# Three PSUM banks for scores and two for row maxima in a macaron block

## The reference

```python
x = x + 0.5 * ffn(layernorm(x), W_up, W_gate, W_down)      # 256 -> 1024 -> 256
x = x + attn(layernorm(x), Wq, bq, Wk, bk, Wv, bv)
x = x + 0.5 * ffn(layernorm(x), W_up, W_gate, W_down)

def ffn(x, W_up, W_gate, W_down):           # weights ternary: clip(round(W/s), -1, 1) * s, s = mean|W|
    return (silu(x @ up.T) * (x @ gate.T)) @ down.T

def attn(x):                                # 16 heads of 16, 4 key/value groups, causal
    q, k, v = ...                           # k and v shared by the 4 heads of a group
    scores = q @ k.T / sqrt(16), -inf above the diagonal
    return softmax(scores) @ v
```

## Time and profile before

| | |
|---|---|
| time, median of 3 runs | 612.36 us (611.18 to 612.61) |
| span of the profiled execution | 610.4 us (its own time is not given beside it; median minus span is 2.0 us) |
| PE busy | 566.9 us, 93% |
| DVE busy | 485.1 us, 79% |
| ACT busy | 411.1 us, 67% |
| POOL busy | 184.6 us, 30% |
| TensorE clock granted | 0.997 of full, mean over the span |

### The profile page before, as it was taken

How to read it: one execution, slowest core, us unless ns; L and a number is a source line. 1 busy time by engine, 2 the same in 40 slices (tenths; PEclk the granted TensorE clock), 3 DMA queues, 4 the chain that set the end, 5 groups by cost and what they waited for, 6 DMA issues and landing times.

```text
span 610.4 us, 12447 instructions
## 1 busy us (share of the span) xinstructions
PE 566.9 (93%) x4276; PEld 346.0 (57%) x4276; DVE 485.1 (79%) x1854; ACT 411.1 (67%) x776; POOL 184.6 (30%) x231
## 2 busy tenths in 40 slices
PE   2869999999989989999899989998899999999998
PEld 2336566555656855656565656554445655666665
DVE  6998978989866889888988987888298687856654
ACT  4637765765635368898889888887866656665741
POOL 3115101110510234555545454557731011101100
PEclk9999999999989999999999999999999999999999
DMA  8601001100205161414141424230111111211112
GB/s 317 207 18 36 18 19 35 35 19 18 36 8 119 24 134 55 91 54 91 55 90 56 91 62 88 84 58 4 36 35 34 53 53 36 69 50 56 35 35 70
DMA packets 71679, 37.90 MB, mean 62 GB/s; under 512 B 33984, under 2 KB 71104, under 8 KB 71616
## 3 DMA queue, kind: packets, MB, share of 16 engines
q1 hardware_dynamic: 71616, 37.11, 23.9%
HBM read 18.22 MB, written 10.49 MB: 47 GB/s over the span
## 4 chain that ended last, share of the span: by engine, by line
PE 79%; DVE 12%; ACT 6%; issue 2%; DMA 1%; DVEq 0%
PE bank L1107 32%; PE bank L1119 17%; PE bank L1206 7%; PE bank L1270 6%; PE bank L1261 5%; PE bank L1233 5%; PE bank L1284 2%; PE bank L1275 2%; DVE hl L847 2%; ACT shared L587 2%; DVE sm_out L969 2%; DVE hid L832 2%; DVE stats L711 1%; PE bank L1098 1%; PE bank L1244 1%
## 5 line engine op out<-in xcount | busy, mean ns | idle before, releaser
L969 DVE CUSTOM_DVE_ANT_0 sm_out<-bank,mask 128x256 f16<-128x256 f32 (+1 forms) x512 | 153.0, 352 | 28.3 <-PE bank L1233 26.4
L477 ACT ACTIVATE silu<-bank,w_scale 128x512 f32<-128x512 f32 x128 | 87.3, 682 | 117.5 <-PE bank L1107 117.5
L832 DVE SCALAR_TENSOR_TENSOR hid<-silu,h_unit,bank 128x512 f32<-128x512 f32 x128 | 95.0, 742 | 63.4 <-ACT silu L477 63.2
L587 ACT ACTIVATE shared<-bank,qk_scale 128x512 f32<-128x512 f32 x192 | 121.2, 675 | 22.7 <-PE bank L1261 22.0
L1119 PE MATMUL bank<-wT_down,hh 128*128 128x256 f16 x512 | 118.7, 273 | 5.5 <-DVE hl L847 5.3
L1119 PE MATMUL bank<-wT_down,hl 128*128 128x256 f16 x512 | 118.7, 273 | 0.0
L847 DVE TENSOR_TENSOR hl<-hid,hh 128x512 f16<-128x512 f32 x128 | 102.9, 804 | 0.0
L1107 PE MATMUL bank<-xh,wT_gate 128*128 128x512 f16 x256 | 97.1, 379 | 4.8 <-DVE hid L832 4.8
L409 POOL TENSOR_TENSOR xnl<-xn,xnh 128x1024 f16<-128x1024 f32 x14 | 30.1, 2150 | 233.9 <-ACT xn L514 199.0
L1107 PE MATMUL bank<-xh,wT_up 128*128 128x512 f16 x256 | 98.0, 383 | 1.2 <-DVE xl L776 1.2
L1107 PE MATMUL bank<-xl,wT_up 128*128 128x512 f16 x256 | 97.9, 383 | 0.0
(11 more groups left out here) (113 smaller groups left out, 751.3 us busy)
## 6 DMA issues: line engine op xcount, KB each, us to landing
q_st<-q_scratch SPq DMA_DIRECT2D x32, 256.0 KB
q_scratch<-q_hl SPq DMA_DIRECT2D x16, 256.0 KB, 2.2
out_dram<-x SPq DMA_DIRECT2D x7, 512.0 KB, 2.9
x<-in_x_dram SPq DMA_DIRECT2D x1, 3072.0 KB, 15.8
k_scratch<-k_hl SPq DMA_DIRECT2D x16, 128.0 KB, 2.4
k_st<-k_scratch SPq DMA_DIRECT2D x16, 128.0 KB
x<-in_x_dram SPq DMA_DIRECT2D x2, 512.0 KB, 4.4
shared<-in_w_up_t_dram SPq DMA_DIRECT2D x2, 512.0 KB, 6.1
```

The costliest lines, as they stand in the source:

```text
L477: act.activation(silu[:, e % 2, :], U[e % 2][:, :], ACT.Silu, scale=w_scale[:, 0:1]).then_inc(silu_ready, 1)
L587: act.activation(prob[:, place % 2, i, :], ST[(3 * place + i) % 2][:, :], ACT.Exp, scale=qk_scale[:, 4:5]).then_inc(exp_done, 1)
L832: dve.scalar_tensor_tensor(out=hid[:, e % 4, :], in0=silu[:, e % 2, :], scalar=h_unit[:, 0:1], in1=GT[e % 2][:, :], op0=ALU.mult, op1=ALU. ...
L969: ins = dve.tensor_tensor_reduce(sm_out[:, i, cols], SM[i][:, cols], mask[:, S - size:S], 1.0, MASKED, ALU.add, ALU.max, rowmax[:, seq_par ...
```

## The change

The same eight banks are given out otherwise. The scores have three, ST[0] to ST[2], one for each part; a part waits for the exp three parts back (`exp_done` at m-2). The maxima have two, SM[m % 2], and a part waits for the reduction two parts back (`sm_done` at m-1). Which physical bank each is changes with it (bank 0 and 2 for the maxima, 1, 3 and 4 for the scores). At the end of the first stage, `max_scores` is called in two pieces: parts 0 and 1 where all three stood, part 2 after the down half that follows, and for head-group 3 behind the projections and a down half.

```diff
--- before.py
+++ after.py
@@ -127,7 +127,7 @@
 
         bank = [ctx.enter_context(nc.psum_tensor(f"bank{i}", [P, 512], F32)) for i in range(8)]
         U, GT, ACC, TR = bank[0:2], bank[2:4], bank[4:6], bank[6:8]
-        SM, ST, PV, MI = bank[0:3], bank[3:5], bank[5], bank[6:8]
+        SM, ST, PV, MI = (bank[0], bank[2]), (bank[1], bank[3], bank[4]), bank[5], bank[6:8]
         MT = PV[:, S:2 * S]
         FIRST_MT = ST[0][:, 0:S]
 
@@ -584,7 +584,7 @@
 
                 for i in parts:
                     act.wait_ge(st_ready, 3 * n + i + 1)
-                    act.activation(prob[:, place % 2, i, :], ST[(3 * place + i) % 2][:, :], ACT.Exp,
+                    act.activation(prob[:, place % 2, i, :], ST[i][:, :], ACT.Exp,
                                    scale=qk_scale[:, 4:5]).then_inc(exp_done, 1)
 
             def attention_pair(pair, last):
@@ -966,7 +966,7 @@
                 for j in heads:
                     cols = slice((j - heads[0]) * size, (j - heads[0] + 1) * size)
                     h = HPG * g + j
-                    ins = dve.tensor_tensor_reduce(sm_out[:, i, cols], SM[i][:, cols], mask[:, S - size:S], 1.0, MASKED,
+                    ins = dve.tensor_tensor_reduce(sm_out[:, i, cols], SM[(3 * n + i) % 2][:, cols], mask[:, S - size:S], 1.0, MASKED,
                                                    ALU.add, ALU.max, rowmax[:, seq_par, qt, h:h + 1])
                     if j == heads[-1]:
                         ins.then_inc(sm_done, 1)
@@ -1181,14 +1181,18 @@
                         if t == 0:
                             pe.wait_ge(st_loaded[0][0], 16 * N_ST)
                         if t < 3:
-                            max_scores(t, 0, t)
+                            max_scores(t, 0, t, range(2))
                     if t > 1:
                         down_half(NC - 1, 1, t, 0)
+                    if ph == 0 and t == 3:
+                        max_scores(3, 0, 3, range(2, 3))
                     down_half(NC - 1, 1, t, 1)
                     if ph == 0:
+                        if t < 3:
+                            max_scores(t, 0, t, range(2, 3))
                         if t == 2:
                             max_transposes(0, 0, 0)
-                            max_scores(3, 0, 3)
+                            max_scores(3, 0, 3, range(2))
                         if t < 3:
                             project_all(1, t)
 
@@ -1225,12 +1229,12 @@
 
                 par, at = k // 2 % 2, k % 2 * S
                 for i in parts:
-                    if not (isinstance(n, int) and n == 0):
-                        pe.wait_ge(sm_done, 3 * n + i - 2)
+                    if 3 * n + i > 1:
+                        pe.wait_ge(sm_done, 3 * n + i - 1)
                     heads = range(HPG) if i == 2 else range(2 * i, 2 * i + 2)
                     size, rows = (P, at) if i == 2 else (S, at + P)
                     for j in heads:
-                        ins = pe.matmul(SM[i][:, (j - heads[0]) * size:(j - heads[0] + 1) * size],
+                        ins = pe.matmul(SM[(3 * n + i) % 2][:, (j - heads[0]) * size:(j - heads[0] + 1) * size],
                                         q_st[:, par, HPG * g + j, rows:rows + P],
                                         k_st[:, par, g, at:at + size],
                                         start=True, stop=True)
@@ -1252,13 +1256,13 @@
                     pe.wait_ge(mx_loaded[g // 2], 32 * (b + 1))
                 at, heads = seq * S, slice(HPG * g, HPG * (g + 1))
                 for i in parts:
-                    if not (isinstance(n, int) and n == 0 and i < 2):
-                        pe.wait_ge(exp_done, 3 * n + i - 1)
+                    if n:
+                        pe.wait_ge(exp_done, 3 * n + i - 2)
                     if i < 2:
                         keys, queries = at, q_st[:, par, HPG * g + 2 * i:HPG * g + 2 * i + 2, at:at + S]
                     else:
                         keys, queries = at + P, q_st[:, par, heads, at + P:at + S]
-                    pe.matmul(ST[(3 * (4 * k + g) + i) % 2][:, :], k_st[:, par, g, keys:keys + P], queries,
+                    pe.matmul(ST[i][:, :], k_st[:, par, g, keys:keys + P], queries,
                               start=True, stop=True).then_inc(st_ready, 1)
 
             def outputs(n, k, g):
```

## The result

The changed kernel takes 618.46 us (median of 4 runs, 617.95 to 618.90) where the kernel before takes 612.49 (611.18 to 614.02, 4 runs): a ratio of 1.011, interval 1.0095 to 1.0124. Six microseconds slower, and 0.4 above the forecast of 618.1. The profiled execution has a span of 617.0 us (before: 610.4) and took 618.71 in all, so 1.7 us lie around the span.

What follows compares the result with a forecast made beforehand. No engine alone sets the pace; PE, DVE and ACT hold each other through PSUM banks. 2.3 + 3.4 + 0.0 = +5.7 us on a span of 610.4 gives 616.1, plus 2.0 around it 618.1 us; range 611 to 623.5.

Steps and rivals of the forecast that it cites:

- the named signs: New profile: PE's waits for ACT before scores under 3 us, for DVE 8 or more, longer stretches, later projection and first scores.
- The lead-in: End of first stage to steady part: maxima 2 wait for DVE, delaying projection and first scores; +2.3 us, bounds 0 to 2.9.
- The six stretches: Eight-head-group stretches ahead of the last pair: +0.75 us each for three with Newton steps, +0.4 for three without; +3.4.
- The last pair: End of attention, no projections between: waits for DVE replace waits for exp; sum 0.0 us, bounds -2 and +1.
- -0.18 three or four times: Last pair: scores 2 come 1.48 us after maxima 0 where the exp let them come at 1.66.
- +0.2 to +0.4 twice or three times: Last pair: loss in us where four transposes stand between maxima 2 and scores 2.
- the term of -0.6: Last five groups, without maxima: outputs then only beat ACT's copy, worth 0.15 us a group, four times.
- The 1.05 us ahead of scores at 428.44: Last five groups, without maxima: this PE wait for the exp of part 0 goes.
- The exp wait as the true limit: Rival, attention stage: maxima have air, about half of PE's 12.2 us of stops returns, -6, 606 us; chance 0.12.
- The waits do swap: Rival: the waits just swap, 0.88 us at 333.47 against 0.37, lead-in absorbed; 611 to 614 us, chance 0.14.
- DVE as the bound: Rival: every new wait lands and delays DVE's next feed, so lags add up; 627 us, chance 0.12.
- The rule of the Trainium skill: Repeating bubbles on the engine that should be full can mean too little PSUM; before scores, it says a third bank is missing.

Runs made afterwards that it cites:

- experiment 4: Changed kernel with maxima part 2 issued behind scores part 2 of the same group, in the steady part and last pair: 612.75 us, ratio 1.0004.
- 7: Changed kernel with DVE reducing only 128 of each head's 256 columns in maxima part 0: 611.5 us, ratio 1.0004.
- 8: Kernel before with DVE reducing only 128 of each head's 256 columns in maxima part 0, as control: 609.31 us, ratio 0.9969.
- experiment 5: Changed kernel with three maxima banks for head-groups 0 to 3 and part 2 of head-group 4 behind the first scores: 615.78 us, ratio 1.0066.
- experiment 2: Changed kernel's banks with the old order, all three maxima parts in one piece: 620.89 us, ratio 1.014.
- 1: Changed kernel with the old banks, so only PE's order at the end of the first stage is new: 611.35 us, ratio 0.9994.
- experiment 3: Changed kernel with scores in two banks and one bank left empty: 620.61 us, ratio 1.0133.

## Why the prediction was right, step by step

**The mechanism.** Maxima 2 wait for DVE's maxima 0, and hold scores 2 behind them: shown by experiment 4, which turns round only the order of the two and gets more than 5 us back, and by 7 against 8. Most of the named signs came: no PE wait for ACT ahead of scores (under 3 us were allowed), 11.7 us of PE and 32.0 of PEld for DVE (8 or more). One came only by half: the stretch without Newton steps was to grow from 29.4 us to 29.8, and it was 28.98 from marker to marker and grew to 29.16.

**The lead-in, +2.3 forecast, +2.6 measured, 2.3 of it its own.** The second head-group's wait stands where it was walked (PE timeline of the changed kernel, from 205 us):

```profile
205.32 0.40 PE L1237 MATMUL bank<-k_st,q_st 128*128 128x128 f16 x4 [1.07 <-DVE rowmax L969]
205.55 1.95 PE L1210 MATMUL bank<-xT,wqkv 128*128 128x256 f32 x8
...
217.26 0.40 PE L1237 MATMUL bank<-k_st,q_st 128*128 128x128 f16 x4 [1.34 <-DVE rowmax L969]
...
218.20 0.82 PE L1265 MATMUL bank<-q_st,k_st 128*128 128x512 f16 x3
```

The projection starts at 205.55 (forecast 205.1), the first scores at 218.20 (217.8). Both are 0.4 late, and 0.30 of that stood there at the first maxima, before the change acts. The rest is DVE's own pieces ahead of maxima 0, which had moved by another 0.1: the walk took DVE's end of 204.83 from before as fixed. Without the 0.30 the lead-in costs 2.29 at the head of the steady part, as forecast. That it is a separate loss is shown by experiment 5.

**The six stretches, +3.4 forecast, +2.7 measured.** The walk inside one was right: relative to the V transposes at its head, the eight output transposes at the end of a stretch without Newton steps come 0.53 us later than before (340.06 - 309.93 against 335.19 - 305.59); forecast was 335.65, +0.46. The step that failed is the start of it. I took each stretch as beginning level with PE, but in the steady state ACT is behind already at its head, by the same rows at each: the eight output transposes stand 0.96 us behind the V transposes and not 0.62.

```profile
280.71 1.09 PE L1288 MATMUL bank<-ident,shared 128*128 128x128 f32 x8 [0.18 <-ACT shared L617]
```

(279.75 to 280.71; before, 334.57 to 335.19.) Of 0.53 at the end 0.34 were there at the head, which leaves 0.19 a stretch: what was measured. With Newton steps it is 0.95 - 0.34 = 0.61 against 0.75. The first stretch gained 0.96, and 0.44 of it is a wait for a load that the kernel before hasn't got:

```profile
229.11 0.39 PE L1237 MATMUL bank<-k_st,q_st 128*128 128x256 f16 x2 [0.44 <-DMA q_st<-q_st]
```

**The last pair, 0.0 forecast, +1.0 measured**, the far end of its bounds. First, the forecast didn't follow from its own terms: -0.18 three or four times, +0.2 to +0.4 twice or three times and -0.6 lie between -0.9 and +0.1, with -0.5 in the middle. Second, the +1.0 is made of three parts:

- Behind the last transposes of maxima the term of -0.6 was right. From them to the first matmul of the second feed-forward stage it takes 9.87 us before (425.68 to 435.55) and 9.22 or 9.23 in experiments 2, 4, 5 and 7, which have three score banks and no lower clock there: -0.65. In the changed kernel's profile it takes 9.62 (432.22 to 441.84), since it has the lower clock from 433.8 to 437.1. So 0.4 us of this profile are the clock's and not the banks'.
- Ahead of them the steps add 1.24 us instead of about +0.1, and 0.73 of that is a wait for a load that the kernel before hasn't got there:

```profile
405.91 0.39 PE L1237 MATMUL bank<-k_st,q_st 128*128 128x256 f16 x2 [0.73 <-DMA q_st<-q_st]
```

- The other 0.5 are spread over the groups; where they come from stays open.

The loads of Q and K for the last sequences (L242 to L246) are issued by SP behind the two that carry the row maxima into q_st (L254), and these wait for the maxima. SP's queue, before:

```profile
391.70 1.31 SPq L254 DMA_DIRECT2D q_st<-mx_hl  x2
397.22 0.63 SPq L244 DMA_DIRECT2D k_st<-k_scratch  x1
398.24 0.68 SPq L246 DMA_DIRECT2D q_st<-q_st  x1
```

and after:

```profile
397.67 1.31 SPq L254 DMA_DIRECT2D q_st<-mx_hl  x2
403.18 1.33 SPq L244 DMA_DIRECT2D k_st<-k_scratch  x1
404.89 0.69 SPq L246 DMA_DIRECT2D q_st<-q_st  x1
```

L254 moved by 5.97 us, where PE's V transposes moved by 5.30: the maxima's lag on DVE, 0.67, goes through SP's queue into the loads for PE. The last of these moved by 6.65, because the issue of L244 took 1.33 us and not 0.63. So only half of its lateness is the maxima's. The stop comes in every kernel with two maxima banks in the steady part and in none with three (before, 1, 8), but in these profiles its size doesn't follow the lag of L254: with a lag of 0.67 it is 0.73, 0.87 (experiment 2) and 1.19 (5), and with none it is 0.39 (3). This is read from the traces; no run took that wait away alone.

The 1.05 us ahead of scores at 428.44 went as forecast. At 432.22 PE stands 1.8 us ahead of the transposes of the last maxima (before, 0.72). The profile names no releaser, but DVE's last read for them ends 0.09 us earlier (432.05 + 0.08), as before (425.50 + 0.08, PE at 425.68).

**Sum.** 2.6 + 2.7 + 1.0 + 0.3 behind the stage = 6.6 on the span, against 5.7. The 0.3 behind the stage had no term in the forecast, and it comes with the third score bank: from the first matmul of the second feed-forward stage to the end of the span it is 175.1 to 175.2 us in all kernels that have it and 174.8 to 174.9 in the others (before, 1, 3, 8). The 2.0 us around the span were too many: executions whose time and span are both given have 1.7 or 1.8, and 2.0 came from the span of one execution and the median of others. At a like clock the change costs 5.9 us, of 5.7 forecast. The good total owes something to errors that cancel: the stretches were put 0.7 too high, the last pair some 0.6 too low (without the lower clock), the end 0.3.

**The rivals.** The exp wait as the true limit fails by the result, and experiment 3 gives it its size: with it gone the kernel gains nearly 4 us beside two maxima banks, not 6, and the two maxima banks take nearly 10. The waits do swap in PE's sum (12.2 for 11.7), but not in time, since one of them stands ahead of more. DVE as the bound: its idle before maxima did grow, 24.9 to 28.3, but the stretches stay at 29.16 and 30.18 throughout, so lags don't add up from stretch to stretch; they repeat. The rule of the Trainium skill (Perfetto Trace Analysis, Optimization Strategy) pointed at a real shortage, a bank for scores, and experiment 3 puts it at nearly 4 us; followed by taking a bank from the maxima it loses 6.

## What to carry to other kernels

The idle time ahead of an instruction says where a queue stood, not what taking it away gives: ask which engine was busy then, and if it was the one that sets the end, less comes (here nearly 4 us of 12.2). A bank taken from one pair of engines is paid for where its user lags and something needed sooner is queued behind it in order; before buying a bank, try issuing the waiting instruction last (here more than 5 us without a bank or an instruction more). When a periodic stretch is walked, start it from the lag that it will have in the steady state, and follow the late data through the DMA queue too. Before medians are subtracted, look at the mean clock of the executions in each: here it moved a difference of 3.85 us to 2.15, and one of 5.75 to 7.0.

## What was not expected

- Scores in a third bank are worth nearly 4 us of 612 though PE had stood 12.2 us for them.
- The same cut of DVE's work is worth three times as much (5.75 against 1.9 us at a like clock) where PE's order hangs on it.
- A lag of 0.67 us on DVE's side crossed SP's queue of DMA issues, grew to 1.35 us there by one slow issue, and came back as a 0.73 us stop of PE, 8 us later.
- A reduction of half as many columns is not half as long: 128x256 takes 0.42 us, 128x128 0.29 us in the changed kernel's DVE timeline, so some 0.16 us of each don't go with its columns (estimate from the two rows: 0.29 - (0.42 - 0.29)).
